# Other prices in the order of an attention kernel: score hops, waiting tanh operations, earlier feed

## The reference

```python
x = x + layernorm(attention(layernorm(x)))     # 16 heads of 16, causal, w_attn and w_proj with LoRA
x = x + layernorm(ffn(layernorm(x)))           # 3 blocks
# a block of ffn: y = linear(h); y = gelu(layernorm(y)); h = linear(y) + h
```

## Time and profile before

| what | us |
|---|---|
| median of 3 runs | 1263.21 (1259.63 to 1264.57) |
| the profiled execution | 1261.49 |
| its span, first to last instruction | 1259.5 |
| TensorE busy | 1213.4 |
| ScalarE busy | 1097.8 |
| VectorE busy | 754.9 |
| GpSimd busy | 437.9 |

### The profile page before, as it was taken

How to read it: one execution, slowest core, us unless ns; L and a number is a source line. 1 busy time by engine, 2 the same in 40 slices (tenths; PEclk the granted TensorE clock), 3 DMA queues, 4 the chain that set the end, 5 groups by cost and what they waited for, 6 DMA issues and landing times.

```text
span 1259.5 us, 30041 instructions
## 1 busy us (share of the span) xinstructions
PE 1213.4 (96%) x11429; PEld 526.9 (42%) x11429; DVE 754.9 (60%) x1820; ACT 1097.8 (87%) x1251; POOL 437.9 (35%) x1373
## 2 busy tenths in 40 slices
PE   8999999999999999999999999999999999999957
PEld 6556434343343433444334334343344333333246
DVE  6775225577765666766665675756666665551066
ACT  4765999999999998999999999999899999999922
POOL 3221235343433552345334253432323431220044
PEclk9999999999999999999999999999999999999989
DMA  5985644644435453454443443543435343331000
GB/s 170 314 307 174 191 122 119 187 150 132 140 102 151 123 143 86 126 164 135 123 122 102 122 119 107 137 118 107 137 86 158 110 129 102 89 93 47 1 5 17
DMA packets 144208, 159.48 MB, mean 127 GB/s; under 512 B 76326, under 2 KB 106044, under 8 KB 144060
## 3 DMA queue, kind: packets, MB, share of 16 engines
q1 hardware_dynamic: 139772, 153.26, 41.0%
q10 hardware_dynamic: 4288, 4.26, 1.1%
HBM read 117.62 MB, written 35.65 MB: 122 GB/s over the span
## 4 chain that ended last, share of the span: by engine, by line
PE 68%; ACT 7%; DVE 5%; issue 3%; DMA 3%; POOL 2%; SPq 2%; ACTq 0%; POOLq 0%; DVEq 0%
PE O L1500 30%; PE S L1482 21%; PE F L209 15%; ACT probs L1425 6%; SPq L595 2%; DMA feed_mem<-turns 2%; DMA qkv_mem<-turns 1%; DVE feed_mem L1703 1%; PE S L1571 1%; DVE feed_mem L1704 1%; DVE o_turned L1652 1%; PE S L1555 0%; POOL rstdC L1385 0%; DVE stC L1594 0%; DVE feed_mem L1727 0%
## 5 line engine op out<-in xcount | busy, mean ns | idle before, releaser
L1425 ACT ACTIVATE probs<-S 128x1024 f32<-128x1024 f32 x1056 | 995.2, 1050 | 65.1 <-PE S L1482 56.1
L1500 PE MATMUL O<-probs,vg 128*32 128x512 f32 (+3 forms) x4608 | 523.9, 564 | 5.3 <-DVE o_turned L1652 3.4
L1482 PE MATMUL S<-q_op,k_op 64*128 64x512 f32 (+3 forms) x2304 | 383.9, 425 | 9.9 <-ACT probs L1425 8.2
L1482 PEld LDWEIGHTS S<-q_op,k_op 64*128 64x128 f32 x2304 | 186.5, 184 | 324.2 <-ACT probs L1425 235.3
L1500 PEld LDWEIGHTS O<-probs,vg 128*32 128x32 f32 x4608 | 120.7, 110 | 208.6 <-issue 177.8
L1403 POOL TENSOR_SCALAR_AFFINE_SELECT probs<-probs 128x512 f32<-128x512 f32 (+1 forms) x160 | 92.9, 590 | 164.6 <-ACT probs L1425 164.0
L1373 POOL TENSOR_SCALAR tmpC<-mvC 128x2 f32<-128x2 f32 x84 | 24.4, 290 | 309.3 <-DVE rstdC L1603 307.4
L209 PE MATMUL F<-wfT,feed_mem 128*32 128x256 f32 x1280 | 83.5, 388 | 3.1 <-DVEq L1637 1.5
L1652 DVE STREAM_TRANSPOSE o_turned<-O 128x512 f32<-128x512 f32 x32 | 22.8, 712 | 97.1 <-PE O L1500 96.1
L1704 DVE SCALAR_TENSOR_TENSOR feed_mem<-feed_mem 128x512 f32<-128x512 f32 x90 | 65.9, 732 | 3.1
L1703 DVE SCALAR_TENSOR_TENSOR feed_mem<-feed_mem 128x512 f32<-128x512 f32 x90 | 63.6, 707 | 3.5 <-DVE qkv_mem L1709 0.5
(11 more groups left out here) (210 smaller groups left out, 1254.7 us busy)
## 6 DMA issues: line engine op xcount, KB each, us to landing
k_op<-qk_rows SPq DMA_DIRECT2D x256, 256.0 KB, 3.7
qk_rows<-parts SPq DMA_DIRECT2D x32, 512.0 KB, 4.4
q_op<-qk_rows SPq DMA_DIRECT2D x128, 128.0 KB, 2.9
turns<-feed_mem SPq DMA_DIRECT2D x160, 64.0 KB, 1.9
feed_mem<-turns SPq DMA_DIRECT2D x40, 256.0 KB, 2.9
k_op<-qk_rows SPq DMA_DIRECT2D x48, 128.0 KB, 2.6
x_in<-in_L_attn_x ACTq DMA_DIRECT2D x8, 512.0 KB, 5.3
feed_mem<-in_L_attn_x SPq DMA_DIRECT2D x16, 256.0 KB, 3.5
```

What stands on the lines that cost most here:

```text
L1425: nc.scalar.activation(probs[:, n % NP, :, :], S[:, n % NS, :, :], ACT.Exp, scale=SCALE).then_inc(exp_ok, 1)
L1482: last = nc.tensor.matmul(S[:, n % NS, a, at:at + TT - q0], k_op[mine, c % RING, pair, k0:k0 + P], q_op[mine, v % QS, pair, q0:TT], start= ...
L1500: last = nc.tensor.matmul(O[h * STRIP:(h + 1) * STRIP, q0:TT], vg[:, kb, col:col + STRIP], probs[:, n % NP, a, at:at + TT - q0], start=fir ...
```

## The change

Only `plan` and its constants are touched; the operations, their buffers and their semaphores stay, and what changes is the order in which each engine issues them.

- `SCORE_OUT` = 0.25 and `SLOT_OUT` = 0.3 take the place of `HOP` between a score and its exponential, and between an exponential and the score that takes its slot. The slack of `next_product` is reckoned with `SCORE_OUT`.
- `THIRD` goes from 0.25 to 0.3, `SLACK` from 0.5 to 0.3, `FEED_EACH` from 62 to 50 (a tile is due every 100 units).
- A tanh of tiles 0 to 6 has rank 2, behind the exponentials, until it has been ready for `GELU_WAIT` = 4 us; then it has rank 0 again.

```diff
--- before.py
+++ after.py
@@ -819,9 +819,11 @@
 ENDING = STEPS[-1]
 FOLDS, FOLD_FROM, FOLD_EACH = 1 + 2 * BLK, 1.0, 3.5
 FOLDED_EARLY = 2
-FEED_FROM, FEED_EACH = 24.0, 62.0
-BATCH, THIRD, SLACK, BACKLOG = 3, 0.25, 0.5, 10
+FEED_FROM, FEED_EACH = 24.0, 50.0
+BATCH, THIRD, SLACK, BACKLOG = 3, 0.3, 0.3, 10
 HOP = 0.15
+GELU_WAIT = 4.0
+SCORE_OUT, SLOT_OUT = 0.25, 0.3
 LANDING = {"k_load": 4.3, "q_load": 4.3, "moved": 1.9, "x_load": 4.2, "store": 3.0, "moved_late": 1.9}
 TURNS = ["_x"] + [str(m) for m in range(BLK)]
 PUTS, GETS = [f"put{x}" for x in TURNS], [f"get{x}" for x in TURNS]
@@ -1085,7 +1087,7 @@
             return score, max(now, mine[score])
         busy = free["ACT"] + sum(us[x] for x, at in ready["ACT"].items() if at <= now + HOP)
         first = score is not None and mine[score] <= now
-        slack = busy - (now + HOP + us[score] + SWITCH["score"]) if first else 1e9
+        slack = busy - (now + SCORE_OUT + us[score] + SWITCH["score"]) if first else 1e9
         pending = sum(1 for z in exp_ends[-8:] if z > now) + scores - len(exp_ends)
         if first and pending >= NS - 1 and can:
             slack = 1e9
@@ -1107,6 +1109,15 @@
     def landing(x):
 
         return LANDING_FIRST if x[0] == "moved" and x[1] < FIRST_MOVED else LANDING.get(x[0], 0.0)
+
+    def hop(a, y):
+
+        return SCORE_OUT if y[0] == "exp" and a[0] == "score" else SLOT_OUT if y[0] == "score" and a[0] == "exp" else HOP
+
+    def rank_now(x, now):
+
+
+        return 2 if x[0].startswith("gelu") and x[1] < NT - 1 and now < ready["ACT"][x] + GELU_WAIT else rank[x]
 
     locked, F_free, blocked = None, 0.0, {}
 
@@ -1125,7 +1136,7 @@
             kind, shape = kind_of(x), shape_of(x)
         else:
             start = now
-            x = min((x for x, at in ready[e].items() if at <= now), key=lambda x: (rank[x], -left.get(x, 0.0), ready[e][x], str(x)))
+            x = min((x for x, at in ready[e].items() if at <= now), key=lambda x: (rank_now(x, now), -left.get(x, 0.0), ready[e][x], str(x)))
         del ready[e][x]
         if takes_bank(x):
             locked = (emptied[x[0]],) + x[1:3]
@@ -1138,7 +1149,7 @@
         for y in users.get(x, []):
             waiting[y] -= 1
             if not waiting[y]:
-                ready[engine[y]][y] = max(end[a] + (0.0 if engine[a] == engine[y] and a[0] not in PUTS else 0.0 if not us[a] else landing(a) if engine[a] == "SP" or a[0] == "moved_late" else HOP) for a in after[y])
+                ready[engine[y]][y] = max(end[a] + (0.0 if engine[a] == engine[y] and a[0] not in PUTS else 0.0 if not us[a] else landing(a) if engine[a] == "SP" or a[0] == "moved_late" else hop(a, y)) for a in after[y])
                 if takes_bank(y):
                     if locked is not None:
                         blocked[y] = ready["PE"].pop(y)
```

## The result

| | before | changed |
|---|---|---|
| median | 1262.99 | 1254.25 (1253.16 to 1256.68, 4 runs) |
| ratio | | 0.994, interval 0.992 to 0.996 |
| span of the profiled execution | 1259.5 | 1252.4 |
| exponentials end | 1196.0 | 1188.2 |
| after them | 63.5 | 64.2 |

The account below looks back on a forecast made before the run. Mutual waits of 65 to 80 us between TensorE and ScalarE, running neck and neck, were taken as the bound. Terms -13 + 9 - 4 - 3 + 4 = -7, taken as -9, gave 1254 against the median; range 1238 to 1274.

Parts of the forecast that it names:

- the slower case: Rival on TensorE: batches split and two or three scores alternate, +13 us, 1276; chance 0.25.
- SLACK and SCORE_OUT, -13: ScalarE's 127 stops lose 0.2 us each, 25 us; half given back for displaced feed pieces on TensorE: -13 us.
- More batches, +9: On TensorE, batches that start earlier close at two scores; 25 batches more at 0.36 us each: +9 us.
- the gross price: On TensorE, each batch of scores costs 0.36 us for going over and back.
- SLOT_OUT and THIRD, -4: TensorE's waits for a batch's third slot get shorter, between 0 and 13 us: -4 us.
- split batches: Rival: TensorE sets the pace and 70 more batches cost 25 us, +13 in all, 1276; chance 0.25.
- Tanh, -3: On ScalarE, tanh operations that run in stops save between 0 and 22 us, most already absorbed: -3 us.
- Due times, +4: Tile feed done sooner, feedless stretch grows: 3 us of TensorE capacity unused, +1 for a long stop: +4 us.
- The 3.41 us stop: ScalarE's longest stop, laid to a feed product 1.54 us late and three more pieces before the scores.
- The rule on repeating gaps: Gap after each third exponential may mean short buffers (three slots); then order can't remove it and the sum is 0.
- No difference: Rival: three slots and a cycle's mean work set ScalarE's stops, tanh finds no gap; 1263, chance 0.25.
- larger gain: Rival: ScalarE's stops lose 0.3 us each and nothing returns in batches, -28 us, 1235; chance 0.10.

Follow-up runs that it names:

- the batches of two: The kernel before with BATCH 2 instead of 3: 1288.0 us, ratio 1.0205.
- the last list: The kernel before with SLACK 0.35, GELU_WAIT 8, FEED_EACH 60, BACKLOG 9, SCORE_OUT 0.15, SLOT_OUT 0.2 (the list meant to beat both): 1248.27 us, ratio 0.9886.

## Why the prediction was right, point by point

The total, the end of the exponentials (1187 forecast, 1188.2 measured) and the fall of the waits for scores (to about 30, measured 30.2) came out. Some of the steps did not, and their errors cancelled. That the total came within 1 us of the forecast is in part luck: the same rules with due times two units later take 1277.79 us, outside its range. Of the signs that it named, two did not come: the last run of exponentials is not longer than 71 but broken by a tanh 10 us before the end, and the tanh operations are not preceded by more stops (4.6 us ahead of all 42, for 4.2 before). Batches of two did not outnumber those of three either (165 to 239), which was the sign of the slower case.

*SLACK and SCORE_OUT, -13.* Right in mechanism: with `SLACK` and `THIRD` back the waits are 61.0 us in 138, and the time 16 us more. It is not a term by itself, though: alone, the same two constants cost 3.4 us. But `SCORE_OUT` has no part in it; with the hops back at 0.15 the time is the same. And the step "the displaced piece must run in a later cycle, in TensorE's slack" left out where it waits until then. Weighings that are put off keep `probs` slots taken, and ScalarE then waits for those, 15.4 us in 23 waits. That was the wait next in line, and the text didn't name it. It took 14.1 of the 20.3 us won; the half that I gave back for another reason happens to be of that size.

*More batches, +9.* 35 more, not 25. At the net 0.17 us of the batches of two that would be about 6 us, an estimate; but the list with the hops set back has 48 fewer and takes the same time, so a cost of the further batches is not shown in the changed kernel. That part of the gross price hides was left out of the sum.

*SLOT_OUT and THIRD, -4.* Not borne out. Charging the hops cures no stall that matters: TensorE's waits for a slot fall, but from 8.2 us to 4.8, and with the hops back they are 6.5 at the same time of the kernel. Alone the hops cost 0.9%: the list then closes batches early (410 of them) and the stops stay. That is the rival of the split batches. `THIRD` was never changed apart from `SLACK`.

*Tanh, -3.* Its size is not shown: about 2 us in the exponentials with it set back, and no difference that can be told when it is alone (1260.88), both within what a shuffled order does. Its cover was wrong: I had the 66 us between tile 6's end and the attention's hide the longer way of a half. In the changed kernel that cover is gone, and the step about the due times had it grow.

*Due times, +4.* This is the step that failed. "The feed is done sooner and the stretch without it grows" took a due time as if it gave TensorE room. It only orders feed against weighings, and `SLACK` had just taken away the places in which feed went in. The feed ended 57 us later in spite of it. The parts were costed one by one, and these two aren't separable: without the earlier due times the same change is 5.4% slower than the kernel before. For the other half of the step, a cost of their own of about 4 us, there is only the 2.2 us in the kernel before, of the size of chance.

*The 3.41 us stop* was read as a feed product 1.54 us late with three more pieces behind it. The clock of the stretches of the kernel before around it shows what else was in it:

```profile
480.00:483.00 3.00, 3.00 (x34) 1.17 (x30) 0.01 (x1) 3.00 (x4) 0.00 (x0) 1.00 0.90 241
483.00:485.00 2.00, 0.46 (x6) 0.20 (x8) 1.63 (x5) 2.00 (x3) 1.04 (x1) 0.98 0.32 75
485.00:487.00 2.00, 2.00 (x24) 1.23 (x20) 1.90 (x4) 0.47 (x1) 0.00 (x0) 0.50 0.54 132
487.00:488.30 1.30, 1.30 (x16) 0.37 (x8) 1.18 (x2) 0.00 (x0) 0.00 (x0) 0.50 0.00 0
488.30:492.00 3.70, 3.70 (x32) 1.39 (x28) 3.27 (x7) 3.12 (x4) 0.47 (x1) 1.00 0.00 0
```

TensorE had done 0.46 us of work in the two us from 483, and from 484.9 its clock is at 0.50, 1.2 instead of 2.4 GHz, until 488.3; the 32 matmuls took 3.60 us instead of the 1.94 of full clock. About half of that long stop, 1.7 of 3.41 us, is the clock. The kernel before has two such stretches (484.9 and 904.7), the changed one too (279.7 and 477.7), of 3.4 us each, so this doesn't tell the two apart.

*The rule on repeating gaps.* By the Trainium skill, Trace Analysis, Optimization Strategy, a repeating gap can mean too few buffers. The runs agree in one sense only: with the same three slots of `S`, 127 waits became 57 to 80 by order alone, so most of them were not due to the number of score slots; whether a fourth slot would remove the rest was not tried. The gap that took their place is one of buffers, the 12 slots of `probs`; whether more of them would remove it was not tried either.

The rivals: *split batches* came true in direction for the hops alone (1.009) and for batches of two (1.02), not for the whole. *No difference* would have been right for the tanh. A *larger gain* than the forecast exists, as the last list shows (1248.27), but not the rival's 1235, and 6 us of it are lost to the tail.

## What to carry to other kernels

A list that weaves slack work between two engines near their bounds has a second clock to watch: whether the slack work itself is through in time. Before you price a rule that gives it fewer places, work out when the woven work ends and what stands behind it; here a reserve of 66 us went to nothing while the busy times of TensorE's matmuls, ScalarE, VectorE and GpSimd stayed within 5 us, and one step further the chain that was hidden stood alone, with its matmuls at half the clock. When a change turns several constants of a scheduler, set each back from the end as well as putting it in alone, and shift one that has no meaning by a little; that tells what a rule brings from what one order happened to give.

## What the runs showed of the hardware that was not expected

TensorE's clock fell to 1.2 GHz in the middle of a kernel that keeps it busy for 98% of the time, after one pause of under 2 us (1.54 us idle at 484.8, 1.99 at 904.8), and came back 3.4 us later. In the tail of the run without the earlier due times, where products come 11 to 14 us apart, the groups of 32 behind such a pause ran at half speed, 3.64 us for 1.94. By the 3.60 us for 1.94 at 484.8, such a stretch costs about 1.7 us on top of the lateness ahead of it.

But a pause of this length does not always bring one. The changed kernel's TensorE at 1135.2 and that of the run with the hops set back at 715.5:

```profile
1135.21 1.93 PE L1511 MATMUL O<-probs,vg 128*32 128x512 f32 x24 [1.70 <-DVE o_turned L1663]
```

```profile
715.46 1.93 PE L209 MATMUL F<-wfT,qkv_mem 128*32 128x256 f32 x32 [1.74 <-DVEq L1648]
```

The clock is at 1.00 in the two us behind either, and the 32 matmuls at 715.5 take 1.93 us. In the attention of its profiled execution the run with the hops set back has no stretch at half clock, the kernels before and changed have two each, and those with `SLACK` set back and with the hops alone three each. The list that beat both has one of 6.8 us, which begins at 370.3 inside a pause of 2.48 us. Differences of a few us between two of these kernels can lie in that alone.
